# The second norm's reciprocal root: from one GpSimd power to twelve VectorE instructions

## The reference, cut to what matters

```python
h = h + attn(layernorm(h))            # attn ends with: out = a_flat @ Wlt
h = h + ffn(layernorm(h))
def layernorm(x, eps=1e-05):
    return (x - mean(x)) / sqrt(var(x) + eps)
def ffn(x):                           # E=8 experts, K=2 of them per token
    gates = softmax(x @ Wr + br)
    top_vals, top_idx = top_k(gates, 2)
    out = sum over the two experts e of top_vals[e] * (relu(x @ W1[e] + b1[e]) @ W2[e] + b2[e])
```

## Time and profile before

| | us |
|---|---|
| median of 3 runs | 1500.25 (1497.04 to 1500.66) |
| profiled execution | 1500.72 |
| its span, first to last instruction | 1498.9 |
| PE busy | 1399.7 (93% of the span) |
| DVE busy | 1184.3 (79%) |
| ACT busy | 1008.2 (67%) |
| POOL busy | 788.0 (53%) |

### The profile page before, as it was taken

How to read it: one execution, slowest core, us unless ns; L and a number is a source line. 1 busy time by engine, 2 the same in 40 slices (tenths; PEclk the granted TensorE clock), 3 DMA queues, 4 the chain that set the end, 5 groups by cost and what they waited for, 6 DMA issues and landing times.

```text
span 1498.9 us, 32061 instructions
## 1 busy us (share of the span) xinstructions
PE 1399.7 (93%) x7812; PEld 1121.1 (75%) x7812; DVE 1184.3 (79%) x3231; ACT 1008.2 (67%) x2311; POOL 788.0 (53%) x888
## 2 busy tenths in 40 slices
PE   5899999999999999999998988898987999999993
PEld 4677888888888888888886766666765888888871
DVE  2988898989899898989897688777777766666655
ACT  2677887878887888878786666666654555555540
POOL 1675444444444444444442477767666565665561
PEclk8999999999999999999999999999999999999997
DMA  3422222222222222222224988777755787777779
GB/s 85 154 76 73 88 100 76 91 80 87 87 80 91 76 91 80 101 80 91 79 78 144 297 273 273 219 233 227 223 172 198 279 292 254 249 251 246 243 284 362
DMA packets 180725, 245.76 MB, mean 164 GB/s; under 512 B 32641, under 2 KB 143761, under 8 KB 180657
## 3 DMA queue, kind: packets, MB, share of 16 engines
q1 hardware_dynamic: 159872, 206.57, 41.5%
q0 software_dynamic: 13920, 31.33, 6.4%
q10 hardware_dynamic: 6864, 7.09, 1.4%
HBM read 99.85 MB, written 89.51 MB: 126 GB/s over the span
## 4 chain that ended last, share of the span: by engine, by line
PE 70%; DVE 11%; POOL 7%; issue 7%; DMA 2%; ACT 2%; SPq 1%; DVEq 0%; POOLq 0%; ACTq 0%
PE bank L403 15%; PE bank L405 13%; PE bank L404 13%; PE pair_ps L1690 10%; PE bank L1621 5%; PE bank L1715 5%; POOL sorted_scratch L839 5%; PE pair_ps L1854 1%; PE bank L1611 1%; POOL rstdB L833 1%; PE bank L1789 1%; DMA yearly<-y_scratch 1%; PE pair_ps L405 1%; PE pair_ps L403 1%; PE bank L1629 1%
## 5 line engine op out<-in xcount | busy, mean ns | idle before, releaser
L697 POOL TENSOR_TENSOR prob<-expo,inv 92x368 f32<-92x368 f32 x256 | 205.0, 801 | 394.6 <-DVE inv L1219 394.6
L874 POOL DMA_INDIRECT y_scratch<-ytok,tin x198 | 194.0, 980 | 124.1 <-issue 91.9
L839 POOL DMA_INDIRECT sorted_scratch<-trow,posi x184 | 180.2, 979 | 96.0 <-issue 57.5
L1690 PE MATMUL pair_ps<-z,xnT 128*92 128x368 f32 x512 | 201.3, 475 | 0.0
L1212 DVE TENSOR_REDUCE peak<-pair_ps 92x4 f32<-92x368 f32 x256 | 136.1, 532 | 73.2 <-PE pair_ps L1690 73.1
L1403 DVE SCALAR_TENSOR_TENSOR hid_l<-bank,hid_h 128x512 fp32r<-128x512 f32 (+1 forms) x159 | 103.5, 655 | 93.7 <-ACT hid_h L1040 92.7
L914 ACT ACTIVATE z<-bank 128x368 f32<-128x368 f32 x254 | 121.2, 477 | 63.0 <-PE bank L405 55.9
L953 ACT ACTIVATE w2s<-bank 128x368 fp32r<-128x368 f32 x256 | 122.5, 478 | 47.4 <-PE bank L405 43.0
L960 ACT ACTIVATE expo<-cent 92x368 f32<-92x368 f32 x256 | 130.4, 509 | 31.2 <-DVE cent L1224 28.2
L1040 ACT ACTIVATE hid_h<-bank 128x512 fp32r<-128x512 f32 (+1 forms) x159 | 90.5, 569 | 78.9 <-PE bank L405 78.3
L1239 DVE TENSOR_TENSOR w2s<-bank,w2s 128x368 fp32r<-128x368 f32 x256 | 136.2, 532 | 6.0 <-ACT w2s L953 3.1
(11 more groups left out here) (274 smaller groups left out, 3875.3 us busy)
## 6 DMA issues: line engine op xcount, KB each, us to landing
ax_scratch<-val SPq DMA_DIRECT2D x64, 736.0 KB, 3.8
arow<-ax_scratch SPq DMA_DIRECT2D x92, 512.0 KB
w1t<-w1s SPq DMA_DIRECT2D x53, 512.0 KB, 3.2
w2t<-w2s SPq DMA_DIRECT2D x53, 512.0 KB, 3.0
tin<-sorted_scratch SPq DMA_DIRECT2D x46, 260.0 KB
xin<-in_x_dram SPq DMA_DIRECT2D x32, 372.0 KB
ywide<-y_scratch SPq DMA_DIRECT2D x32, 256.0 KB, 7.2
h_scratch<-hP SPq DMA_DIRECT2D x32, 184.0 KB, 5.1
```

Of the source, the lines that this page charges most:

```text
L697: nc.gpsimd.tensor_tensor(prob[:, k % 2], expo[:, k % 2], inv[:, k % 2].unsqueeze(2).to_broadcast([S, HH, S]), ALU.mult).then_inc(prob_kep ...
L839: pool.indirect_dma_start(out=sorted_dram, out_offset=bass.IndirectOffsetOnAxis(ap=posi[:, q, choice, r:r + 1], axis=0), in_=trow[:, q, ch ...
L874: pool.indirect_dma_start(out=y_dram, out_offset=bass.IndirectOffsetOnAxis(ap=tin[:, b, r, D:D + 1].bitcast(I32), axis=0), in_=ytok[:, b % ...
L1690: mm(score_ps[k % 2][0:S, 0:GT], xnT[:, q, b * S:(b + 1) * S], z[:, b, half * HH:(half + 1) * HH, :], start=True, stop=True).then_inc(scor ...
```

## The change

VectorE forms the reciprocal root. A first guess comes from the bits of the variance: as a 32-bit integer it is shifted right by one and subtracted from the constant 0x5F3759DF. Three Newton steps y = y * (1.5 - 0.5 * v * y * y) follow. With the addition of eps these are 12 instructions of 128x4. The first 6 (`guess_root` and one step) stand at j = 4 ahead of block 4 of aT_l, where `keep_var2` stood; the other 6 (`close_root`) stand behind block 4 and ahead of block 5. Eleven of the twelve raise `root_step`, for which VectorE then waits. GpSimd's `root2` is gone. Its fourth and fifth scatter now wait for ACT's copy of the 5th block of the next chunk (`turned(5)`) in place of `rstd2_kept`.

```diff
@@ buffers and semaphores
+ROOT_STEPS = 11
-        sb("behind_tiles", [P, 1072], stack=second)
+        sb("behind_tiles", [P, 1064], stack=second)
+        halved = sb("halved", [P, RT], I32, stack=second)
+        near = sb("near", [P, RT], stack=second)
-   var2_kept
+   root_step
@@ GpSimd
-            def root2(c, q):
-
-                pool_waits((var2_kept, c + 1), (trow_kept, 2 * c - 2), (mask_kept, c - 1))
-                nc.gpsimd.tensor_tensor(rstdB[:, q], varB[:], power[:], ALU.pow).then_inc(rstd2_kept, 1)
-
                 if after_first:
                     scatter(c - 1, 1 - q, 0, 3)
-                root2(c, q)
-                if after_first:
-                    scatter(c - 1, 1 - q, 3, 5, (rstd2_kept, c + 1))
+                    scatter(c - 1, 1 - q, 3, 5, turned(5))
                     scatter(c - 1, 1 - q, 5, 2 * RT, turned(AC))
@@ VectorE
-            def keep_var2(c):
+            root_no = [0]
+
+            def root_link(c, ins):
+
+                root_no[0] += 1
+                ins.then_inc(root_step, 1)
+                dve.wait_ge(root_step, ROOT_STEPS * c + root_no[0])
+
+            def guess_root(c, q):
+                root_no[0] = 0
                 at_least(dve, square_kept, 2 * c + 2)
-                at_least(dve, rstd2_kept, c)
-                V.tensor_scalar(varB[:], varB[:], EPS, None, ALU.add).then_inc(var2_kept, 1)
+                at_least(dve, trow_kept, 2 * c - 2)
+                root_link(c, V.tensor_scalar(varB[:], varB[:], EPS, None, ALU.add))
+                root_link(c, V.tensor_scalar(halved[:], varB[:].bitcast(I32), 1, None, ALU.logical_shift_right))
+                root_link(c, V.tensor_scalar(rstdB[:, q].bitcast(I32), halved[:], -1.0, float(0x5F3759DF), ALU.mult, ALU.add))
+
+            def refine_root(c, q):
+                y = rstdB[:, q]
+                root_link(c, V.tensor_tensor(near[:], y, y, ALU.mult))
+                root_link(c, V.scalar_tensor_tensor(near[:], near[:], -0.5, varB[:], ALU.mult, ALU.mult))
+                return V.scalar_tensor_tensor(y, near[:], 1.5, y, ALU.add, ALU.mult)
+
+            def close_root(c, q):
+                root_link(c, refine_root(c, q))
+                refine_root(c, q).then_inc(rstd2_kept, 1)
@@ VectorE, chunk
                     if j == 4:
-                        keep_var2(c)
+                        guess_root(c, q)
+                        root_link(c, refine_root(c, q))
                     if more and 0 < j < HL:
                         keep_aTl(c + 1, j)
 ...
+                    if j == 4:
+                        close_root(c, q)
                     if j == 5:
```

More of the change, by code:

```diff
@@ L366, in build @@
             "aT_done", "aTh_kept", "aTl_kept", "proj_done", "h1_kept"))
-        wrc_done, wrc_kept, lean_kept, square_kept, var2_kept, rstd2_kept, shift_kept = (sem(n) for n in (
-            "wrc_done", "wrc_kept", "lean_kept", "square_kept", "var2_kept", "rstd2_kept", "shift_kept"))
+        wrc_done, wrc_kept, lean_kept, square_kept, root_step, rstd2_kept, shift_kept = (sem(n) for n in (
+            "wrc_done", "wrc_kept", "lean_kept", "square_kept", "root_step", "rstd2_kept", "shift_kept"))
         route, mask_kept, gap_kept, gapexp_kept, count_done, posi_kept = (sem(n) for n in (
@@ L1270, in keep_h1 @@
                 V.tensor_tensor(h1[:, q], proj_ps[:], hch[q][:], ALU.add).then_inc(h1_kept, 1)
-            def keep_var2(c):
-                at_least(dve, square_kept, 2 * c + 2)
-                at_least(dve, rstd2_kept, c)
-                V.tensor_scalar(varB[:], varB[:], EPS, None, ALU.add).then_inc(var2_kept, 1)
+            root_no = [0]
[5 more added lines that the diff above has]
+                root_no[0] = 0
+                at_least(dve, square_kept, 2 * c + 2)
+                at_least(dve, trow_kept, 2 * c - 2)
[10 more added lines that the diff above has]
+                refine_root(c, q).then_inc(rstd2_kept, 1)
+                assert root_no[0] == ROOT_STEPS, root_no
             step_no = [0]
```

## The result

The changed kernel took 1515.05 us (median of 4, 1510.96 to 1516.26) against 1499.78 before (median of 4; the 1500.25 further up is that of the first three), a ratio of 1.010 (95% interval 1.0076 to 1.0124). That is slower by 15.3 us; 17 were forecast, 1517 with a range of 1504 to 1531. The profiled execution took 1514.29 us with a span of 1512.5, 13.6 us longer than the span of before.

What follows compares the result with a forecast made beforehand. The prediction took a ring between POOL and DVE, 12.84 us a chunk, to bound the kernel. Chunks 1 to 8 (+4.2 us), 9 to 20 (+10.8) and ends (+2.0) gave +17.0: 1517 us, range 1504 to 1531.

Steps and rivals of the forecast that it cites:

- The ring: Routing part, once a chunk: POOL's power, DVE's expert choice and positions, three scatters, POOL's next power; 12.84 us.
- Pitch of a linked instruction: DVE's new root instructions: 0.20 us from start to start where the next waits on a semaphore.
- Rival 2: DVE's root instructions: links free once in a row, 0.08 us each, 1485 us in all; chance 0.09.
- V = 3.6: DVE's stretch from the start of `varB` to the next `shift`, forecast at 3.6 us a chunk.
- the 0.12 put in for that: Three scalar-operand instructions among the twelve: none to three held 0.17 us each by scatters, taken as 0.12.
- R unchanged: DVE's stretch from `shift` to the start of `varB`: stays 9.57 us written out, 10.02 in the loop.
- Sum: Whole kernel: +4.2 us for chunks 1 to 8, +10.8 for 9 to 20, +2.0 at the ends; +17.0.
- Half clock: Rival: PE idles before projections 4 and 5 and drops to half clock; 1530 us, chance 0.11.
- POOL some 3 us idle a chunk: Sign of a right forecast: POOL, left with 10.2 us of scatters, idles some 3 us a chunk.
- The new gates of the scatters: Two scatter calls wait for aT_h copies in place of the root; a later start up to 3 us is hidden.

Runs made afterwards that it cites:

- pool_first: The kernel before with GpSimd's power behind one scatter of the chunk before in place of three: 1493.76 us, ratio 0.996.
- six_linked: The changed kernel with six more 128x4 VectorE instructions between guess and first Newton step, a wait behind each: 1550.17 us.
- six_free: The changed kernel with six more 128x4 VectorE instructions between guess and first Newton step, no wait among them: 1525.75 us.
- old_gate: The changed kernel with the fourth and fifth scatter waiting for the root again, as in the kernel before: 1515.8 us.
- before_h_first: The kernel before with h1 (the residual addition) ahead of the next chunk's first aT_l block: 1498.61 us, ratio 0.999.

## Why the prediction was right

Point by point, by its steps:

- *What bounds the kernel.* The ring, as it was read. These rows of the kernel before lie between the earlier trace rows's `shift` at 882.23 and 894.88, and close it: `posi` ends at 889.37, the first of three scatters starts 0.81 us later, the power follows the third at once, `shift` the power.

```profile
889.20 0.17 DVE L1358 CAST posi<-posf 128x8 int32<-128x8 f32 x1
```

```profile
889.12 0.59 POOL L827 DMA_DIRECT2D sorted_scratch<-h1tok  x1
890.18 0.99 POOL L839 DMA_INDIRECT sorted_scratch<-trow,posi  x1 [0.47 <-issue]
...
893.74 1.04 POOL L833 TENSOR_TENSOR rstdB<-varB,power 128x4 f32<-128x4 f32 x1
```

  POOL's own queue comes close behind. Its usual gap between scatters is 0.30 us; ahead of a chunk's first scatter it was 0.47 in the chunks with the ninth DMA (line 827), and 0.78 to 1.43 in the loop, so the queue is 0.2 us shorter than the ring there and 0.5 to 1.1 us in the loop. pool_first, which takes two scatters out of the ring, shows how close that is: its chunks still took 12.51 and 12.35 us.
- *Pitch of a linked instruction*, 0.20 us: measured 0.20 in every chunk looked at. Rival 2, free links, is out by six_linked against six_free.
- *V = 3.6*: 3.64 written out and 3.73 in the loop. The two are that close partly by luck: written out, a held instruction of the scalar-operand kind makes some chunks 3.74 (`varB` took 0.43 us at 893.75) and leaves the others near 3.55; in the loop chunk above none of the three was held (0.17 to 0.18 each), so the 0.12 put in for that wasn't there; in its place came 0.15 us ahead of the first aT_l block and 0.09 ahead of the second, which I had not priced.
- *R unchanged*: 9.51 against 9.58, 10.00 against 10.13.
- *Sum.* By the starts of `shift`, chunks 1 to 8 grew from 101.07 to 104.76 us, +3.7 (+4.2 forecast), and 9 to 20 from 153.63 to 164.59, +11.0 (+10.8 forecast). Chunk 0's V went from 1.69 to 3.47, +1.8 as forecast. Chunks 21 and 22 together lost 1.6 us, where the forecast had +0.2: V of chunk 21 did fall from 4.40 to 3.49 and that of chunk 22 rise from 1.79 to 2.86, but R of chunk 21 fell from 11.28 to 9.61 besides. Most of that fall, 1.49 of 1.67 us, is a half clock of the kernel before which the forecast took to stay: PE had waited 2.96 us for that chunk's mask, the granted clock then stood at 0.85 (1115 to 1120) and 0.80 (1120 to 1125), and from `count` to the end of h1's turn PE took 4.51 us. The changed kernel takes 3.02, at 1.00 (1130 to 1135); the rows of both stand below. What lies ahead of the first `varB` was 0.8 us shorter and what follows the last `shift` 0.4. 3.7 + 11.0 + 1.8 - 1.6 - 0.8 - 0.4 = 13.7, the 13.6 of the span. The 15.3 between the medians lies within the spread of the runs.

```profile
1117.67 0.29 PE L1779 MATMUL bank<-mask_line,before_r 128*128 128x40 f32 x1 [2.96 <-DVE upto L1330]
...
1120.24 1.94 PE L1773 MATMUL pair_ps<-turnw,h 128*128 128x137 f32 x8
```

```profile
1132.09 0.29 PE L1800 MATMUL bank<-mask_line,before_r 128*128 128x40 f32 x1 [0.63 <-DVE upto L1348]
...
1134.02 1.09 PE L1794 MATMUL pair_ps<-turnw,h 128*128 128x137 f32 x8
```

- *Half clock*: not in the changed kernel's loop. The two chunks of before that had it (R of 10.44 and 11.04 in the loop, one in the earlier trace rows) are gone, which hides about 1.5 us of the cost in the loop; that they went was not forecast. six_linked shows the price where it does come: 5 us over the loop.
- *POOL some 3 us idle a chunk.* Shown by this row of the changed kernel's POOL timeline, the first scatter of a chunk, beside waits of about 1.05 ahead of the sixth:

```profile
1026.36 0.97 POOL L837 DMA_INDIRECT sorted_scratch<-trow,posi  x1 [2.91 <-issue]
...
1033.48 0.96 POOL L837 DMA_INDIRECT sorted_scratch<-trow,posi  x1 [1.05 <-ACT aT_f L988]
```

- *The new gates of the scatters* cost nothing: old_gate.

What stays open: why the loop adds 0.15 us ahead of an aT_l block behind a linked instruction, which was not tried by itself, and what exactly brings the half clock on.

## What to carry to other kernels

Moving work off a busy queue pays only by what the receiving engine's chain costs at that place. Count the new instructions by their linked pitch (here 0.20 us, not the 0.08 at which those without a wait follow each other), put them beside the wait that they replace, and look for a shorter formula before the move: twelve instructions lost 1.0%, seven gained 0.4%, and seven with an earlier h1 1.1%. Where a queue is nearly as long as the ring, both must be shortened: the ring alone gave 0.4% (pool_first), and time taken out beside the ring gave nothing (before_h_first).

## What the runs showed of the hardware that was not expected

- The length of a wait alone doesn't tell when the half clock comes. In six_linked it came behind PE waits of 1.87 and 0.56 us (977.00, 979.01) and of 1.83 and 0.34 (993.86, 995.60), but not behind 1.84 and 0.36 (1009.49, 1011.24); in the kernel before it came behind 0.66 and 0.81 (1051.78, 1053.49), and in the changed kernel 0.66 and 0.36 left the clock at 1.00. A VectorE chain 1.2 us longer so cost 1.53 us a chunk (35.1 us in 23).
- A scalar-operand instruction of 128x4 that takes 0.17 us took up to 0.43 while GpSimd issued a scatter (`varB` at 893.75, in a scatter that ran from 893.24 to 894.21; it ended at 894.18, when that scatter did). Begun earlier in a scatter it wasn't held: the one at 891.80 in the kernel before, 0.33 us into a scatter of 0.97, took 0.17.
